# Seeding the bias of a projection in PSUM from ScalarE instead of a TensorE product

## The reference, cut to what matters

```python
x_hat = (x - mean) / sqrt(var + 1e-5)
q = x_hat @ Wq + bq;  k = x_hat @ Wk + bk
v = x_hat @ Wv + bv;  skip = x_hat @ Wskip + bskip
# ... attention over 200000 edges, gelu, layer norm, a graph router, 4 experts
```

## Time and profile before

| | |
|---|---|
| median of 3 runs | 3935.41 us (3935.12 to 3939.36) |
| profiled execution, whole | 3934.06 us |
| its span, first to last instruction | 3932.3 us |
| busy in the span: PE, DVE, ACT, POOL | 85%, 84%, 65%, 64% |
| end of `prepare`: last table (L456) / first gather of the next stage (L762) | 296.9 us / 298.2 us |

### The profile page before, as it was taken

One profiled execution on the slowest core, in us unless ns is written; L12 is line 12 of the kernel. 1 busy time (PEld: TensorE's weight loads), 2 busy tenths in 40 slices (PEclk: granted clock), 3 DMA queues, 4 the chain that ended last, 5 costly groups with the idle time before them and its releaser, 6 DMA issues. The chain is left out here.

```text
span 3932.3 us, 106711 instructions
## 1 busy us (share of the span) xinstructions
PE 3355.5 (85%) x26264; PEld 2475.4 (63%) x26265; DVE 3287.6 (84%) x8768; ACT 2575.0 (65%) x6779; POOL 2500.4 (64%) x2631
## 2 busy tenths in 40 slices
PE   7998999999999999999999983588888888887622
PEld 3446888888788888788888863455555555555422
DVE  8787999999999999999999988676766666666448
ACT  4547888888788888788888866455555555554311
POOL 0007777777777777677777732377777777777760
PEclk9998999999999999999999995599999999999755
DMA  6648888888888888888888856211111111111148
GB/s 208 227 164 248 253 255 261 257 254 257 248 260 254 260 259 257 245 251 255 258 259 256 258 182 228 63 28 33 31 31 33 33 29 33 33 28 32 23 72 336
DMA packets 369514, 683.50 MB, mean 174 GB/s; under 512 B 70326, under 2 KB 243202, under 8 KB 368898
## 3 DMA queue, kind: packets, MB, share of 16 engines
q0 software_dynamic: 157888, 427.05, 39.5%
q1 hardware_dynamic: 178566, 217.28, 16.3%
q10 hardware_dynamic: 32444, 32.10, 2.7%
HBM read 588.41 MB, written 87.78 MB: 172 GB/s over the span
## 5 line engine op out<-in xcount | busy, mean ns | idle before, releaser
L762 POOL DMA_INDIRECT KV<-kv_d,src_i x1564 | 1478.7, 945 | 816.5 <-issue 468.5
L1425 POOL DMA_INDIRECT re_src<-src_tab_d,rsrc x1024 | 985.3, 962 | 312.3 <-issue 245.2
L1026 PE MATMUL agg_ps<-msg,oh 128*128 128x264 f32 x3512 | 890.8, 397 | 1.8 <-DVE agg_ps L844 1.8
L1026 PEld LDWEIGHTS agg_ps<-msg,oh 128*128 128x128 f32 x3512 | 633.3, 190 | 86.8 <-ACT oh L935 2.0
L979 PE MATMUL Q<-q,ohT 128*128 128x256 bf16 x5328 | 662.1, 274 | 1.6
L921 ACT ACTIVATE square<-iota_b,off 128x128 bf16<-128x128 bf16 x1784 | 569.2, 392 | 0.3
L861 DVE TENSOR_REDUCE lg<-prod 128x32 f32<-128x1024 f32 x443 | 540.4, 1220 | 15.3
L849 DVE TENSOR_TENSOR msg<-KV,weigh_ps 128x1056 f32<-128x1056 f32 x439 | 542.5, 1236 | 8.1 <-issue 6.9
L857 DVE TENSOR_TENSOR prod<-KV,Q 128x1024 f32<-128x1024 f32 x443 | 532.7, 1203 | 18.0 <-POOLq L753 9.1
L979 PEld LDWEIGHTS Q<-q,ohT 128*128 128x128 bf16 x5328 | 492.7, 98 | 62.8 <-issue 0.4
L1654 PE MATMUL ex_y_ps<-ex_w,ex_hid 128*112 128x256 f32 x1792 | 441.2, 390 | 0.0
(11 more groups left out here) (289 smaller groups left out, 5578.7 us busy)
## 6 DMA issues: line engine op xcount, KB each, us to landing
q<-q_d SPq DMA_DIRECT2D x446, 192.0 KB
y_d<-ex_y ACTq DMA_DIRECT2D x56, 448.0 KB
KV<-kv_d,src_i POOLq DMA_INDIRECT x1564
rg_ye<-y_d SPq DMA_DIRECT2D x5, 3584.0 KB, 24.4
re_src<-src_tab_d,rsrc POOLq DMA_INDIRECT x1024
nu_xs<-xs_d SPq DMA_DIRECT2D x6, 2688.0 KB, 12.1
kv_d<-pr_kv SPq DMA_DIRECT2D x49, 260.0 KB, 2.2
xs_d<-pr_xs SPq DMA_DIRECT2D x49, 256.0 KB, 2.3
```

What stands on the lines that cost most here:

```text
L762: pool.indirect_dma_start(out=KV[:, t % (KVR * G), :], out_offset=None, in_=k.kv_d, in_offset=bass.IndirectOffsetOnAxis(ap=k.src_i[:, t:t ...
L1026: m = pe.matmul(agg_ps[:, 0:HEADS * HW], oh32[ring(s, 2)][:, t, :], msg[ring(s, 2)][:, t, :, :].rearrange("p h e -> p (h e)"), start=False ...
L1425: pool.indirect_dma_start(out=gs[:, t % (RING * RG), :], out_offset=None, in_=k.src_tab_d, in_offset=bass.IndirectOffsetOnAxis(ap=k.rsrc[: ...
```

## The change

The product of the bias parts goes. Instead the four bias rows are loaded to all 128 partitions (`bias`, four broadcasts of 128 x 256 fp32, placed behind the weights and ahead of the next part of x in SP's queue), and for each tile ScalarE copies 512 fp32 columns of them into the tile's `kv_ps` bank (`kv_bias`) and 512 into its `qs_ps` bank (`qs_bias`). All products then accumulate onto that. Four opening products (identity by weights, one for each bank) stand once at the start of TensorE's program. The ScalarE and GpSimd steps that split the biases and the three DMAs that gathered them go too. `lowest(w-1)` moves ahead of the key copy in `evacuate(w)`, because the bank that tile w + 1 needs is the one that it reads.

```diff
@@ SP
                 for i in range(4):
-                    sp.dma_start(b_row[:, i * D:(i + 1) * D], biases[i].unsqueeze(0)).then_inc(ok["b_in"], 16)
                     sp.dma_start(w_sb[:, :, i * D:(i + 1) * D], ...).then_inc(ok["w_in"], 16)
+                for i in range(4):
+                    sp.dma_start(bias[:, i * D:(i + 1) * D], bc(biases[i].unsqueeze(0), [P, D])).then_inc(ok["b_in"], 16)
@@ PE
                 def project(bank, p, at):
-                    pe.matmul(bank[:, :], ones3[:, :], b_parts[:, at:at + 2 * D], start=True, stop=False)
                     for c in range(2):
-                        m = pe.matmul(..., start=False, stop=(c == 1))
+                        m = pe.matmul(..., start=False, stop=(c == 1), skip_group_check=True)
...
                     pe.wait_ge(ok["xt"], w + 1)
-                    if w == 0:
-                        pe.wait_ge(ok["b_ready"], 48)
-                    if w >= 2:
-                        pe.wait_ge(ok["kv"], w - 1)
+                    pe.wait_ge(ok["kv_biased"], w + 1)
                     project(kv_ps[p], p, 0)
                     if w:
                         less_hi(w - 1)
-                    if w >= 2:
-                        pe.wait_ge(ok["skip"], w - 1)
-                        pe.wait_ge(ok["lo"], w - 1)
+                    pe.wait_ge(ok["qs_biased"], w + 1)
                     project(qs_ps[p], p, 2 * D).then_inc(ok["products"], 1)
...
+                for bank in (*kv_ps, *qs_ps):
+                    m = pe.matmul(bank[:, :], k.ident[:, :], w_sb[:, 0, 0:512], start=True, stop=True)
+                m.then_inc(ok["opened"], 1)
@@ ACT
+                def kv_bias(w):
+                    act.copy(kv_ps[w % 2][:, :], bias[:, 0:2 * D]).then_inc(ok["kv_biased"], 1)
+
+                def qs_bias(w):
+                    act.copy(qs_ps[w % 2][:, :], bias[:, 2 * D:4 * D]).then_inc(ok["qs_biased"], 1)
...
                     act.copy(xs[w % LOOP][:, D:2 * D], qs_ps[p][:, D:2 * D]).then_inc(ok["skip"], 1)
+                    if w:
+                        lowest(w - 1)
                     act.copy(kv[s][:, 0:D], kv_ps[p][:, 0:D])
+                    if w and w + 1 < NW:
+                        act.wait_ge(ok["lo"], w)
+                        qs_bias(w + 1)
...
                 def tile(w):
                     if w + 1 < NW:
                         turned(w + 1)
+                    if 2 <= w + 1 < NW:
+                        act.wait_ge(ok["kv"], w)
+                        kv_bias(w + 1)
...
                         evacuate(w)
-                        if w:
-                            lowest(w - 1)
...
+                act.wait_ge(ok["b_in"], 64)
+                act.wait_ge(ok["opened"], 1)
+                for w in range(2):
+                    kv_bias(w)
+                    qs_bias(w)
                 turned(0)
```

More of the change, by code:

```diff
@@ L151, in prepare @@
         w_sb = sb("pr_w", [P, 2, 4 * D], F32)
[L152 to L155, removed]
+        bias = sb("pr_bias", [P, 4 * D], F32)
         xs = [sb(f"pr_xs{i}", [P, 2 * D], F32) for i in range(LOOP)]
@@ L168, in prepare @@
                  "ends_in", "sort", "flipped", "copied",
-                 "w_in", "b_in", "b_rounded", "b_rest", "b_ready", "stats", "norm", "sqrt",
+                 "w_in", "b_in", "opened", "kv_biased", "qs_biased", "stats", "norm", "sqrt",
                  "xn", "turned", "xt", "products", "kv", "skip", "hi", "less_hi", "mid", "less_mid", "lo")
@@ L246, in _ @@
                 pool.memset(eps[:, :], EPS).then_inc(ok["made"], 1)
-                pool.memset(ones3[:, :], 1.0).then_inc(ok["made"], 1)
-                pool.wait_ge(ok["made"], 3)
+                pool.wait_ge(ok["made"], 2)
                 pool.affine_select(out=k.ident[:, :], in_=k.ident[:, :], compare_op=ALU.not_equal, fill=1.0,
@@ L261, in _ @@
                 pool.iota(k.iota_b[:, :], [[1, P]], base=0, channel_multiplier=0, allow_small_or_imprecise_dtypes=True).then_inc(ok["made"], 1)
[L262 to L265, removed]
             @block.vector
@@ L382, in _ @@
                 d.on(v.tensor_scalar(dst_i[:, :], r_ends[:, 1, :], SRC_BITS, KEY_BASE, ALU.logical_shift_left, ALU.bitwise_or))
-                v.wait_ge(ok["made"], 15)
+                v.wait_ge(ok["made"], 14)
                 d.on(v.tensor_scalar(odd[:, :], odd[:, :], 1, None, ALU.bitwise_and))
@@ L459, in _ @@
             def _(pe):
-                pe.wait_ge(ok["made"], 4)
+                pe.wait_ge(ok["made"], 3)
                 pe.wait_ge(ok["w_in"], 64)
@@ L480, in project @@
                 def project(bank, p, at):
-                    pe.matmul(bank[:, :], ones3[:, :], b_parts[:, at:at + 2 * D], start=True, stop=False)
                     for c in range(2):
-                        m = pe.matmul(bank[:, :], xt[p][:, c, :], w_sb[:, c, at:at + 2 * D], start=False, stop=(c == 1))
+                        m = pe.matmul(bank[:, :], xt[p][:, c, :], w_sb[:, c, at:at + 2 * D], start=False, stop=(c == 1), skip_group_check=True)
                     return m
@@ L627, in _ @@
                 held = []
-                act.wait_ge(ok["made"], 4)
+                act.wait_ge(ok["made"], 3)
                 root(0)
-                act.wait_ge(ok["b_in"], 64)
-                act.copy(b_part[0][:, :], b_row[:, :]).then_inc(ok["b_rounded"], 1)
                 for w in range(3):
                     normalise(w)
[L634 to L638, removed]
+                act.wait_ge(ok["b_in"], 64)
[3 more added lines that the diff above has]
+                    qs_bias(w)
                 turned(0)
```

## The result

| | before | changed |
|---|---|---|
| median of 6 runs, us | 3935.65 | 3915.78 |
| range, us | 3934.5 to 3939.36 | 3913.08 to 3921.82 |
| profiled span, us | 3932.3 | 3911.3 |
| first instruction of the next stage, us | 297.53 | 280.76 |

The ratio is 0.9949, interval 0.9939 to 0.9959: about 20 us faster, 16 to 24. A later set of runs of the same kernel gave 0.9960 (0.9947 to 0.9974). The forecast was 3920, with a gain of 14.65 us from the first stage alone. In the profile the stage gave 16.8 us, 21.0 in all, so 4.2 lie in stages that hold no changed line. The first gather of the next stage came at 281.40 instead of 298.18; 283.5 had been forecast.

A forecast was written before the change was run, and what follows sets the result against it. TensorE and VectorE's sort were both taken as near the first stage's bound. Gains of 7.55 us to the first flip and 7.1 behind it, 14.65 in all, took 3934.06 to 3919.4, stated as 3920; 8-in-10 range 3914 to 3930.

The forecast's parts named there:

- tile 7's scales: Before the first flip: TensorE waits 4.52 us for VectorE's scales, so whatever it gains in tiles 0 to 4 is lost.
- what VectorE waits above 0.75: At the flips: 0.75 us is the bare round trip; only wait above it can be won, 10.93 us at the first.
- both gaps: TensorE's gaps behind the turn (0.10 us) and `less_hi` (0.09): without them a tile saves 0.83 us; 0.75 taken.
- The bare weight load: Rival: weight loads stand unhidden behind the turn and `less_hi`; a tile saves only 0.63 us, total 3922, chance 0.14.
- The wide loads: Four bias broadcasts, 0.52 MB ahead of x's second part, delay the sort and tile 7's scales by 1.5 us.
- The late copies: In tiles 5 and 9 long ScalarE instructions make `qs_bias` late by about 1.1 us each, 2.2 us together.
- The copies: Two ScalarE copies of 512 columns, SBUF to PSUM, per tile: 0.53 us occupancy each, 0.65 until seen, hidden in plain tiles.
- slack of `middle`: In a plain tile `middle` is seen at 3.7 us and TensorE wants it at 3.95: 0.25 us to spare.
- The twelfth flip: Late in the first stage: gain of 0.87 us, limited by VectorE's wait above 0.75.
- The later stages: Stages behind the first hold none of the changed lines and were costed at nothing.
- ScalarE as the bound: Rival: a PSUM copy occupying 1.15 us or more makes ScalarE decide; at 1.3 about 8 us slower, 3943, chance 0.07.
- The round trip: Rival: waiting for ScalarE's copies replaces the product, stretching tiles 0.1 to 0.25 us; total 3927 to 3930, chance 0.21.

The follow-up runs named there:

- products of 64 and 96 rows: Kernel before with its 3-row bias product made 64 or 96 rows by zero rows: 3933.79 and 3917.91 us, tiles 4.90 and 4.31 us, one run each.
- 128 rows throughout: Kernel before with its 3-row bias product padded with zero rows to 128: 3923.43 us, ratio 0.9961, tile 4.30 us.
- the loads alone: Kernel before with only the four broadcast bias loads added, read by nobody: 3940.55 us, ratio 1.0008.
- a third copy: Changed kernel with one further ScalarE copy of 512 columns, SBUF to SBUF, in every tile: 3920.94 us, ratio 0.9962.
- the second profile: Profile of the unaltered changed kernel run again in a later set: 3919.58 us, ratio 0.9960, next stage begins at 282.22 us.

## Why the prediction was right, and where it was off

- **The bound and the place of the gain.** As predicted: nothing before tile 7's scales counts, the first flip gives about half, later flips only what VectorE waits above 0.75.
- **The tile.** "If both gaps go, a tile saves 0.83 ... I take 0.75": it saved 1.03, above my upper end. The step that failed is the reading of the group of four matmuls. I took its 1.82 us as work. Four spacings are 1.72, and the 0.10 left over belonged to the product that I was removing. I had even divided (1.82 - 0.11) / 4 when arguing against the bare weight load and did not ask what the 0.11 was. The products of 64 and 96 rows show whose it is.
- **The bare weight load** (3922, chance 0.14), for which a section of the Trainium skill stood ("TensorE: Matmul & The Clock Gate", Part 3, The mechanism). The trace shows the reverse: with 128 rows throughout, each load starts one product ahead (68.50 for the product at 68.61) and no gap is left; it is the loads round the product on fewer rows, which does use different rows, that start only with their own product (70.42 for the product at 70.43). The loads that were not hidden stood in the kernel before, and went with the product.
- **The wide loads.** 1.5 us at full bandwidth; measured 1.94 at the scales, 2.4 with the loads alone. The five profiles with the loads ahead of x have VectorE's start on x's last part at 31.49 to 31.91, the nine others at 28.87 to 30.02, so of a single difference about half a microsecond either way is chance.
- **The late copies.** Tile 6: 1.1 said, 65.84 - 60.91 - 3.88 = 1.05 measured. Tile 10: 1.1 said, 6.76 - 3.88 - 0.33 = 2.55 measured, and 4.2 at half clock. I had taken over the lateness of the kernel before and reckoned with the bias copy alone. But `less_hi`, ahead of it, now waits 1.42 us for ScalarE's copies: TensorE is ready for it at 77.69 + 1.72 = 79.41, 1.83 us earlier than before (81.24), while ScalarE begins `evacuate` at 80.22, 0.20 us later than before. Behind the first flip: 0.23 us for the bias copy and 0.36 for `middle` (0.3 and 0.3 said).
- **The copies.** 0.53 us of occupancy said, 0.52 measured; slack of `middle` 0.25 said, and a third copy, about 0.5 us more, took it away.
- **The sum.** To the first flip 7.55 said, 8.69 measured: 15 x 1.03 = 15.4, less 1.94 and 1.05 and 2.55, leaves 9.9; the rest, about 1.2, went into tiles with table rows, where `less_mid` starts 0.03 to 0.05 us late behind `middle` (4.25 where the parts give 4.21), and into tile 5, which gained only 6.56 - 6.31 = 0.25 us: behind the longer wait it ran at a granted clock of 0.61 instead of 0.74. Behind it 7.1 said, 8.1 measured. The twelfth flip gave 1.69 where I said 0.87: VectorE has table steps of its own there, which cover the bare round trip, so all of its wait of 1.62 could go, not what stood above 0.75. At the end, 3919.4 + 1.35 is 3920.8 and not 3920, a slip of 0.8.
- **Luck in the sum.** 8.69 against 7.55 is close in part because errors cancel: 15 tiles at 0.28 more each are 4.2 us, and the loads, the late copies, tile 5 and the table rows took 3.1 of them back. With the second profile's half clock in tile 10 the first flip gains 7.09 and the stage 15.3, where 7.55 and 14.65 were said.
- **The later stages.** "I cost them at nothing": by kernel they are. From the stage's start to the node update's first GpSimd step before took 2067.1 us and the changed kernel 2064.9 and 2067.3 in its two profiles. Of the 4.2 us of the first comparison 2.2 are that spread and 2.8 the clock of 28 products, less 0.8 lost elsewhere.
- **The rivals.** ScalarE as the bound needed a copy of 1.15 us, and it is 0.52. The round trip does hold TensorE in tiles 6 and 10 and behind flips, as priced but for tile 10; in plain tiles it does not, and in those with table rows by 0.05 us at most.

## What to carry to other kernels

Read a matmul's price from the starts on both sides of it, and take the group behind it too: two small products on few rows cost 0.60 us a tile here beside 0.42 us of columns, and padding them with zero rows to full height gained most of what removing them did. Look at the rows of the weight loads as well: a load that starts with its own product is one that nothing hides. When an engine becomes faster, look where it now meets an engine that was never late. A wait there costs itself and, by chance, the clock behind it. A single profile can be 4.5 us lucky in a kernel of 3.9 ms; compare stages and tiles, not spans, and take a second profile before reading a difference of a microsecond or two.

## What the runs showed of the hardware

- A bf16 product on 3 or 64 rows among fp32 products on 128 rows carried three gaps of 0.10 us: ahead of it, behind it, and inside the group behind. On 96 and 128 rows it carried none. The weight loads of the narrow product and of the fp32 product behind it started with their own product (70.42 for 70.43, 70.74 for 70.75), those of full height one product ahead (68.50 for 68.61). Why the border lies between 64 and 96 is open.
- A ScalarE copy of 512 fp32 columns from SBUF to PSUM took 0.64 us and kept the engine for 0.52; from PSUM to SBUF the mean was 0.585.
- ScalarE's copies seeded PSUM banks onto which TensorE then accumulated, ninety-eight times, with right results; one product had written each bank first. What happens without it no run shows.
- Equal waits of 1.42 and 0.68 us on TensorE, 0.27 us of work between them, left the clock at 2.4 GHz in one execution (granted clock 1.00 from 77.48 to 84.24) and took it to 1.2 GHz for a stretch in another of the same kernel (0.80 from 77.48 to 85.90, 0.66 from 81.00 to 85.50).
